# Memory attention with 32x32 array tiles for the outputs, a ones column for the softmax sum, and three constant products a step

## What is computed

```python
q, k, v = x @ Wq, x @ Wk, x @ Wv              # x: layernormed latents; 16 query heads of 8
q4 = q.reshape(B, S, 16, 8)
k4 = jnp.repeat(k.reshape(B, S, 8, 8), 2, axis=2)
v4 = jnp.repeat(v.reshape(B, S, 8, 8), 2, axis=2)
probs = softmax(einsum("bsnd,btnd->bnst", q4, k4) / sqrt(8))
a_dot = einsum("bnst,btnd->bsnd", probs, v4)
sigma_q = elu(q.reshape(B, S, 2, 64))
a_mem = (sigma_q @ memory) / (sigma_q @ memory_norm)[..., None]
w = sigmoid(memory_weight)
x = x + a_dot * (1 - w) + a_mem * w
```

## Time and profile before

| | us |
|---|---|
| median of 3 runs | 1138.36 |
| lowest and highest | 1136.80, 1141.94 |
| profiled execution | 1137.78 |
| its span in the trace | 1135.5 |

### The profile page before, as it was taken

One profiled execution on the slowest core, in us unless ns is written; L12 is line 12 of the kernel. 1 busy time (PEld: TensorE's weight loads), 2 busy tenths in 40 slices (PEclk: granted clock), 3 DMA queues, 4 the chain that ended last, 5 costly groups with the idle time before them and its releaser, 6 DMA issues. The chain is left out here.

```text
span 1135.5 us, 37923 instructions
## 1 busy us (share of the span) xinstructions
PE 1001.3 (88%) x13868; PEld 793.3 (70%) x13868; DVE 738.2 (65%) x2792; ACT 734.7 (65%) x1794; POOL 485.9 (43%) x883
## 2 busy tenths in 40 slices
PE   5799999987688769998899999999999998878864
PEld 2678888873677459887678888888888887323343
DVE  3578888875789578995476556556556553473376
ACT  3578888873578528885376766766756754564467
POOL 1122222213655026675066666766666765102042
PEclk9899999999799889999999999999999999998979
DMA  2443333310000455773365445445455442000001
GB/s 61 115 115 78 83 81 77 83 39 1 1 1 2 159 189 187 233 226 99 97 154 144 119 114 144 114 117 137 118 126 133 112 123 68 29 0 0 1 0 38
DMA packets 70699, 105.57 MB, mean 93 GB/s; under 512 B 12560, under 2 KB 50320, under 8 KB 70384
## 3 DMA queue, kind: packets, MB, share of 16 engines
q1 hardware_dynamic: 68080, 98.84, 32.3%
q0 software_dynamic: 2496, 5.12, 1.7%
HBM read 89.12 MB, written 14.79 MB: 92 GB/s over the span
## 5 line engine op out<-in xcount | busy, mean ns | idle before, releaser
L1688 ACT ACTIVATE d_p<-d_p,d_nmax 128x289 f32<-128x289 f32 x256 | 137.1, 539 | 128.3 <-DVE d_nmax L1726 127.5
L1555 POOL TENSOR_TENSOR d_p<-d_p,d_rtotal 128x288 f32<-128x288 f32 x256 | 169.3, 667 | 39.6 <-DVE d_rtotal L1732 35.0
L1726 DVE CUSTOM_DVE_ANT_0 d_p<-bank,d_low 128x289 f32<-128x289 f32 x256 | 109.7, 429 | 79.7 <-PE bank L1609 78.3
L1609 PE MATMUL bank<-x_keyT,d_q 128*128 128x289 f32 x512 | 155.1, 420 | 3.5 <-DVE d_nmax L1726 2.1
L1622 PE MATMUL bank<-d_pT,d_xr 32*128 32x128 f32 x4608 | 137.9, 273 | 1.4 <-ACT rows_out L1697 0.9
L445 ACT ACTIVATE a_p<-a_p,a_nmax 128x257 f32<-128x257 f32 x256 | 116.2, 506 | 33.7 <-DVE a_nmax L482 31.9
L1622 PEld LDWEIGHTS bank<-d_pT,d_xr 32*128 32x128 f32 x4608 | 131.6, 187 | 6.3 <-issue 2.1
L1740 DVE STREAM_TRANSPOSE d_pT<-d_p 128x288 f32<-128x288 f32 x256 | 119.2, 465 | 22.1 <-POOL d_p L1555 19.7
L482 DVE CUSTOM_DVE_ANT_0 a_p<-bank,a_low 128x257 f32<-128x257 f32 x256 | 93.8, 422 | 28.0 <-PE bank L395 26.5
L1609 PEld LDWEIGHTS bank<-x_keyT,d_q 128*128 128x128 f32 x512 | 82.3, 190 | 35.1 <-DVE d_nmax L1726 23.6
L353 POOL TENSOR_TENSOR a_edge<-a_vlast,a_p 128x32 f32<-128x32 f32 x64 | 15.7, 246 | 178.0 <-ACT a_p L445 165.2
(11 more groups left out here) (344 smaller groups left out, 2183.4 us busy)
## 6 DMA issues: line engine op xcount, KB each, us to landing
d_xr<-key_rows SPq DMA_DIRECT2D x256, 144.0 KB, 3.2
d_low<-mask_low SPq DMA_DIRECT2D x64, 144.5 KB, 3.8
a_ctT<-in_ctxT SPq DMA_DIRECT2D x64, 128.5 KB, 2.1
a_low<-mask_low SPq DMA_DIRECT2D x64, 128.5 KB, 3.0
c_ct<-in_ctx SPq DMA_DIRECT2D x32, 256.0 KB
key_rows<-c_ct SPq DMA_DIRECT2D x32, 256.0 KB, 2.3
c_w<-in_L_ffn_w SPq DMA_DIRECT2D x8, 578.0 KB, 10.3
c_w<-expert_out SPq DMA_DIRECT2D x8, 256.0 KB, 4.9
```

The source lines that it names most:

```text
L1555: nc.gpsimd.tensor_tensor(p, p, rtotal[:, b % 2, g:g + 1].broadcast_to([128, EDGE]), ALU.mult).then_inc(normed, 1)
L1609: nc.tensor.matmul(S[u % 2], q[:, b // 4, b % 4, 4 * g:4 * g + 4, :].rearrange("p h q -> p (h q)"), keyT[:, bass.ds(i * EIGHT + b, 1), :]. ...
L1688: nc.scalar.activation(p, p, ACT.Exp, bias=nmax[:, b % 2, g:g + 1], scale=-1.0, accum_out=total[:, b % 2, g:g + 1]).then_inc(exp_made, 1)
L1726: nc.vector.tensor_tensor_reduce(P[:, b % 2, g, 0:KEYS], S[u % 2], low[:, b % 4, :], -1.0, 3.4e38, ALU.add, ALU.min, accum_out=nmax[:, b % ...
```

## The change

In the loop of memory attention:

- The roles of the masks are exchanged: keys are masked by `own_head` and queries by `query_scale`, so that a row of the probabilities belongs to one head group and a column block to another.
- `vb` gives way to `v`, 128 x (2 x 4 x 4 x 9): eight values and a column of ones. `output` becomes 64 products of 32x32 array tiles with 9 columns (4 batches x 4 column tiles x 4 row tiles; the row tiles write banks 4 to 7). Their ninth column is the sum of the exponentials.
- DVE's `normalise` goes. `output` on DVE is now: reciprocal of the sums (16 elements a partition, from PSUM), product with it (128 elements, from PSUM), and a transpose of 32x32 blocks to `aT`. ACT's `masked` goes.
- `transposes` waits for the exponential itself, and one step behind, not two. S has one bank. Three constant products stand ahead of each wait for the exponential.
- The memory branch has fewer banks: NUM and SPREAD share bank 3, DEN and TURNED lie in banks 4 and 5 beside OP. Waits are added for that; SPREAD is due at delay 4 (was 5), the last product at 5 (was 6).

```diff
-            S = [core.bank[:, n, :].rearrange("p (c k) -> p c k", k=LAT) for n in (0, 1)]
-            TP, OP, VP = (core.bank[:, n, :].rearrange("p (b k) -> p b k", b=4) for n in (2, 3, 4))
+            S = core.bank[:, 0, :].rearrange("p (c k) -> p c k", k=LAT)
+            TP, VP = (core.bank[:, n, :].rearrange("p (b k) -> p b k", b=4) for n in (1, 2))
+            OP = core.bank[:, 4:8, 0:4 * (DH + 1)].rearrange("p h (b d) -> p b h d", b=4)
-            NUM, SPREAD = core.bank[:, 5, :], core.bank[:, 7, :]
-            DEN, TURNED = core.bank[:, 6, 0:8], core.bank[0:8, 6, 128:256]
+            NUM, SPREAD = core.bank[:, 3, :], core.bank[:, 3, :]
+            DEN, TURNED = core.bank[:, 4, 256:264], core.bank[0:8, 5, 256:384]
...
-                nc.gpsimd.memset(vb[:], 0.0).then_inc(vb_cleared, 1)
+                nc.gpsimd.memset(v[:], 1.0).then_inc(ones_made, 1)
...
+                def transposes(n):
+
+                    if n >= 1:
                         pe.wait_ge(t_copied, n)
+                    occupied(core, 1, 3)
+                    pe.wait_ge(exp_made, n + 1)
                     for b in range(4):
...
+                def scores(n):
+                    j = n % 2
                     pe.wait_ge(qb_made, n + 1)
-                    if not first:
-                        pe.wait_ge(shifted, n - 1)
+                    if n >= 1:
+                        pe.wait_ge(shifted, n)
...
+                def output(n):
                     pe.wait_ge(t_copied, n + 1)
                     pe.wait_ge(v_copied, n + 1)
-                    if not first:
-                        pe.wait_ge(o_masked, n)
+                    if n >= 1:
+                        pe.wait_ge(o_scaled, n)
+                    c = due(n + 1, 3)
+                    if c is not None:
+                        pe.wait_ge(inverted, c + 1)
+                    c = due(n + 1, 4)
+                    if c is not None:
+                        pe.wait_ge(turned_kept, c + 1)
                     for b in range(4):
-                        ins = nc.tensor.matmul(OP[:, b, :], vb[:, j % 2, b, :], pT[:, j % 2, b, :], start=True, stop=True)
+                        for g in range(4):
+                            for h in range(4):
+                                rows, cols = slice(32 * h, 32 * h + 32), slice(32 * g, 32 * g + 32)
+                                ins = nc.tensor.matmul(OP[cols, b, h, :], pT[rows, n % 2, b, cols], v[rows, n % 2, b, g, :], start=True, stop=True)
                     ins.then_inc(o_made, 1)
...
                 def retrieve(n):
 
+                    if n >= 1 and (due(n, 2) is not None or due(n, 3) is not None):
+                        pe.wait_ge(o_scaled, n)
                     c = due(n, 2)
                     if c is not None:
                         pe.wait_ge(elu_made, c + 1)
                         if c:
-                            pe.wait_ge(num_kept, c)
+                            pe.wait_ge(weighed, c)
                             pe.wait_ge(turned_kept, c)
...
-                    c = due(n, 5)
+                    c = due(n, 4)
                     if c is not None:
                         pe.wait_ge(turned_kept, c + 1)
-                        if c:
-                            pe.wait_ge(weighed, c)
+                        pe.wait_ge(num_kept, c + 1)
...
+                for n in range(GROUPS):
+                    if n >= 1:
+                        transposes(n - 1)
+                    scores(n)
+                    if n >= 1:
+                        output(n - 1)
+                    values(n)
+                    retrieve(n)
+                transposes(GROUPS - 1)
+                output(GROUPS - 1)
...
+                def output(n):
+                    dve.wait_ge(o_made, n + 1)
+                    nc.vector.reciprocal(rtotal[:].rearrange("p (b h) -> p b h", b=4), OP[:, :, :, DH]).then_inc(o_inverted, 1)
+                    dve.wait_ge(o_inverted, n + 1)
+                    if n >= 1:
+                        dve.wait_ge(o_turned, n)
+                    nc.vector.tensor_tensor(orow[:].rearrange("p (b h) d -> p b h d", b=4), OP[:, :, :, 0:DH],
+                                            rtotal[:].rearrange("p (b h) -> p b h", b=4).unsqueeze(3).broadcast_to([128, 4, 4, DH]), ALU.mult).then_inc(o_scaled, 1)
+                    dve.wait_ge(o_scaled, n + 1)
+                    nc.vector.transpose(aT[:, 128 * n:128 * n + 128], orow[:].rearrange("p c d -> p (c d)")).then_inc(o_turned, 1)
...
+                for n in range(GROUPS):
+                    invert(n)
+                    shift(n)
+                    if n >= 1:
+                        output(n - 1)
+                    retrieve(n)
+                    if n % 4 == 3 and n >= 7:
+                        attended((n - 7) // 4)
+                output(GROUPS - 1)
                 attended(NCH - 1)
```

183 lines of the change are left out of this document (58 added, 125 removed).

## The result

The changed kernel took 1148.64 us (median of 8 runs, 1138.74 to 1151.91) against 1138.36 for the kernel before; the ratio is 1.0075, 95% interval 1.0047 to 1.0103. It is slower, by under 1% but beyond the interval, where 1131.0 and "faster" had been forecast, and it lies outside the range. The profiled execution was its fastest, 1138.74 us, so its span hides the loss; the stage shows it. The stage's layernorm starts it and the next stage's ends it.

What follows compares the result with a forecast made beforehand. The loop was taken as bound by a ring of hand-overs, no engine being full. Middle +1.1, head -2.7 and tail -5.7 gave -7.3, so 1138.36 became 1131.0 us; range 1124 to 1141.

Steps and rivals of the forecast that it cites:

- The tail: Loop's end, from the transposes of step 15: 8.4 us against 14.1, one step left open instead of two; 5.7 less.
- The middle: Loop from the transposes of step 3 to those of step 15: 66.45 us against 65.3, 1.1 more.
- The tile block: TensorE's 64 output products of 32x32 tiles in each step, 128 records: taken as 1.05 us.
- the far ends, 0.5 and 4.4: Output block's extremes in us: 0.5 if starts come at 3 ns, 4.4 if every record waits for its tile.
- rival 3: Slower: the output block holds TensorE up, each record waiting for its tile or a fixed interval; 1182 or 1163 us; 7%.
- A plain step: Loop step without the memory branch's waits: next transposes after 4.25 us, or 4.35 in steps 3, 6, 9, 12.
- on the path: In plain steps, the constants lie on TensorE's path by 0.5 us, not in a wait for the exponential.
- The 25 ns floor: Product starts never closer than about 25 ns: output block 3.2 us, kernel +32, 1163 us; within rival 3's 7%.
- The waits: Memory-branch steps: about 1 us for ACT's copy in 4, 7, 10; 0.9 for `weighed` in 5, 8, 11.
- step 13: Loop step near the end of the middle, with SPREAD but no delay: 5.2 us.
- The clip of step 0: DVE's clip in the loop's head: near 2.5 us instead of 5.37, as POOL must pause.
- rival 4: Slower: the clock falls in the loop; three half-speed steps undo the gain, all give +45; 1145 and above, 6%.

Runs made afterwards that it cites:

- e10: e4 with 48 unread products of 32x32 tiles and 9 columns a step in place of the three constant products; ratio 1.0238 to the kernel before.
- e12: e4 with its constants kept and 48 unread products of 32x32 tiles added a step; ratio 1.0028 to the kernel before.
- e4: Changed kernel with 16 block-diagonal products of 128x32 tiles and 36 columns a step in place of 64 small ones; ratio 0.9894 to the kernel before.
- e15: e8 with a second scores bank, no constants, and the next group's scores issued between transposes and outputs; ratio 0.9822 to the kernel before.
- e16: e15 with one masked product on VectorE in place of ScalarE's four value copies; 1115.63 us, ratio 0.9798 to the kernel before.
- e13: Changed kernel with the loops over g and h of its 64 products exchanged; ratio 1.0076 to the kernel before.
- e17: e12 with 96 unread small products a step in place of 48; ratio 1.0587 to the kernel before.
- e6: e4 with each product split into four of 9 columns, so 64 a step, each of 128 rows; ratio 1.0193 to the kernel before.
- e5: The changed kernel run again, unaltered; ratio 1.0108 to the kernel before.
- e3: Changed kernel with only row tile 0 computed, three quarters of the outputs left out; ratio 0.9943 to the kernel before.
- e8: e4 with banks of their own for NUM, SPREAD and DEN/TURNED, without the waits that sharing asked for; ratio 0.9867 to the kernel before.

## Why the prediction was wrong

**The sum's terms held, but for disturbances.** From the layernorm to the transposes of step 3 I forecast 40.3 us; it took 41.4, of which 0.8 is a gap for code. The tail was to end 5.7 us sooner and ended 4.8 sooner, with a gap of 0.5. The middle was to take 66.45 and took 82.2, so 15.75 of the 17.8 us by which the stage missed lie there. (The terms that the forecast lists for the tail add to 8.25 us, not 8.4; that changes nothing here.)

**The tile block**: 1.05 forecast, 1.25 measured, 9.8 ns a record; the far ends, 0.5 and 4.4, and rival 3 are out. A plain step was 4.38 (4.35 forecast). Timeline of step 9:

```profile
340.10 0.60 PE L698 MATMUL bank<-ident,b_p 128*128 128x128 f32 x4
340.54 1.06 PE L707 MATMUL bank<-b_kb,b_qb 128*128 128x128 f32 x8
341.52 1.25 PE L726 MATMUL bank<-b_v,b_pT 32*32 32x9 f32 x128
342.70 1.16 PE L734 MATMUL bank<-wb_wv,b_yg 128*128 128x128 f32 x8
343.70 0.27 PE L754 MATMUL bank<-ident,b_inverse 128*8 128x128 f32 x1
343.81 0.83 PE L56 MATMUL bank<-ident,mean_w 128*128 128x128 f32 x6
```

The constants start with no wait and the transposes (344.48) follow at once: on the path, as forecast, and not in a wait. The 25 ns floor of the Trainium skill ("TensorE: Matmul & The Clock Gate", section "Wait — 56ns, not 53.3ns?"), kept as a rival, holds neither for different tiles (9.8 ns) nor quite for the same one (21 to 22 ns).

**The waits** for ACT's late copy (steps 4, 7, 10: 6.28, forecast 6.2) and for `weighed` (steps 5, 8, 11: 7.11, forecast 7.0) were right; step 13 was not (6.0 without its gap, 5.2 forecast). The clip of step 0 took 2.51 us (forecast 2.5), after 5.37 in the earlier trace rows:

```profile
284.35 2.51 DVE L872 TENSOR_SCALAR b_low<-b_qT 128x512 f32<-128x512 f32 x1
```

**The step that failed is the argument in rival 4**: "PE has work for 4.2 of 4.25 us, and middle and first stage kept the full clock", which gave 6%. I took busy time in the records for what the clock goes by. In e10 and e12 TensorE is busier than in the kernel before, and its clock falls. The price was of the right size: the rival had 3.05 us for a step wholly at half clock, and half clock in parts of four steps cost 8.6 us, more than the whole gain of 7.3. That the first stage kept its clock was weak evidence. Its tile products have nine moving columns, as the changed kernel's have, but 128 rows, and they are a small part of each step of 3.3 us, beside products of 128 and 257 columns (timeline, kernel before):

```profile
191.17 0.72 PE L395 MATMUL bank<-a_kT,a_qb 32*128 32x257 f32 x8
191.85 0.71 PE L417 MATMUL bank<-a_v,a_pT 128*32 128x9 f32 x64
```

What it is in the changed kernel's tiles that lets the clock fall stays open.

**A term was missing**: nobody in the sum paid for the code. The first stage's tiles have 64 loads and as many products in a run, half a packet; the change makes 256 instructions in 1.25 us. The gaps took 5.3 us in the middle, 0.8 in the head and 0.5 in the tail. Without the gaps and the falls, as e4 shows for a block of a quarter of the products, the middle is 64.7 and the stage 112.2, 10.6 under the kernel before; the forecast had 7.3 less.

## What to carry to other kernels

Cutting a product into many small tiles saves nothing that a block-diagonal operand doesn't save with fewer and wider products, and it costs twice more: count the instructions in an unbroken run against the time a packet of code takes, and don't take a high busy share in the records as a promise that the clock holds (e12: busy 27.16 of 30.70 us, then half clock). Fillers for the clock cost about what they give as soon as they are on the path; shorten the wait instead, by putting the next group's independent product into it (e15, e16). And an edit that moves a wait to another engine should be followed once more around TensorE's own order before ScalarE or VectorE is blamed.

## What the runs showed of the hardware

- Small products overlap when neighbours in the stream are in different tiles of the array, whether they differ in rows or in columns (9.3 to 10.2 ns a record with 32x32 tiles and 9 columns, in the changed kernel, e12, e13 and e17); in the same tile they take 21 to 22 ns a record (e6, e10).
- Code arrives in packets of 16 KB, 0.9 to 1.5 us each. A run of 192 fast instructions showed no gap in 16 steps (e12), one of 256 gaps of 0.2 to 2.5 us in four or five of twelve (changed kernel, e5), one of 384 a gap every time, 1.8 to 2.4 us in 15 of 16 (e17). The longest gap of the changed kernel comes at the same record in three traces.
- At the same number of products, the same steps and nearly the same recorded busy time, the granted clock held through 64.7 us with tiles of 128 rows and 36 moving columns (e4) and fell three times with tiles of 32 rows and 9 columns (e3); e8, with e4's tiles and fewer waits, fell once, for 3.4 us.
